# A fused attention, feed-forward, convolution and mixture-of-experts kernel: another order of ScalarE, TensorE and VectorE in the last two pairs of batches, and the last four experts' weights loaded one by one

## The reference, cut to what matters

```python
x = x + jnp.tanh(g_xattn[1]) * _L1_xattn_ref(ctx_2048, ctx_2048, _layernorm(x), L1_xattn_ssm_kernel, L1_xattn_D, 8)
x = x + jnp.tanh(g_ffn[1]) * _L1_ffn_ref(_layernorm(x), gate_w, w_gate_up, w_down, ws_gate_up, ws_down)
...
logits = jnp.einsum('th,eh->te', x, gate_w)          # 2048 rows, 64 experts
scores = jax.nn.softmax(logits, axis=-1)
topk_w, topk_ids = jax.lax.top_k(scores, 6)
topk_w = topk_w / (jnp.sum(topk_w, axis=-1, keepdims=True) + EPS)
...
routed = jnp.einsum('tef,ehf->th', jax.nn.silu(g) * u * comb[:, :, None], w_down)   # F = 176
shared = jnp.einsum('tf,hf->th', jax.nn.silu(sg) * su, ws_down)                     # 352
return routed + shared
```

## Time and profile before

| what | value |
|---|---|
| median of 3 runs | 728.07 us (726.86 to 729.16) |
| the profiled execution: its own time | 728.68 us |
| the profiled execution: span from first to last instruction | 726.9 us |
| mean granted clock of TensorE | 0.946 |
| TensorE busy (matmul) | 610.1 us, 84% |
| VectorE busy | 471.4 us, 65% |
| GpSimd busy | 450.9 us, 62% |
| ScalarE busy | 297.0 us, 41% |
| DMA moved | 163.69 MB, mean 225 GB/s |

### The profile page before, as it was taken

One profiled execution on the slowest core, in us unless ns is written; L12 is line 12 of the kernel. 1 busy time (PEld: TensorE's weight loads), 2 busy tenths in 40 slices (PEclk: granted clock), 3 DMA queues, 4 the chain that ended last, 5 costly groups with the idle time before them and its releaser, 6 DMA issues.

```text
span 726.9 us, 11813 instructions
## 1 busy us (share of the span) xinstructions
PE 610.1 (84%) x3072; PEld 470.3 (65%) x3072; DVE 471.4 (65%) x1596; ACT 297.0 (41%) x657; POOL 450.9 (62%) x512
## 2 busy tenths in 40 slices
PE   4698998769877989898747787999999999999930
PEld 3455554446666877787636566888888888887720
DVE  5898987998369898889764714245445545454425
ACT  3156777958233455455345121232322323233200
POOL 2697845782122478787766715477777777786560
PEclk9899999989999999999978989999999999999975
DMA  7578715869979843854223778899999999996868
GB/s 232 194 251 304 257 46 188 234 179 306 300 272 397 330 162 136 280 184 170 95 88 123 247 237 235 227 251 253 247 244 272 247 256 259 249 280 113 242 97 322
DMA packets 97822, 163.69 MB, mean 225 GB/s; under 512 B 10848, under 2 KB 65568, under 8 KB 96736
## 3 DMA queue, kind: packets, MB, share of 16 engines
q1 hardware_dynamic: 76864, 135.16, 56.6%
q0 software_dynamic: 20608, 27.82, 19.7%
q10 hardware_dynamic: 288, 0.01, 0.0%
HBM read 91.24 MB, written 71.71 MB: 224 GB/s over the span
## 4 chain that ended last, share of the span: by engine, by line
PE 56%; DVE 15%; issue 10%; DMA 7%; POOL 5%; ACT 3%; SPq 3%; DVEq 0%; POOLq 0%; ACTq 0%
PE psum L1159 11%; PE psum L1172 7%; PE psum L1163 5%; PE psum L899 5%; PE psum L1177 4%; PE psum L1043 4%; PE psum L1143 4%; PE psum L973 3%; POOL xs_rows L776 3%; PE psum L941 2%; PE psum L942 2%; PE psum L943 2%; PE psum L871 1%; DVE Z L1956 1%; DVE Z L1957 1%
## 5 line engine op out<-in xcount | busy, mean ns | idle before, releaser
L842 POOL DMA_INDIRECT acc<-hh,toki x128 | 188.0, 1469 | 87.4 <-DVE hh L2168 48.6
L2168 DVE TENSOR_SCALAR hh<-psum,wtok 96x256 f32<-96x256 f32 (+3 forms) x128 | 55.8, 477 | 131.9 <-issue 108.3
L776 POOL DMA_INDIRECT xs_rows<-Z,slot x96 | 100.9, 1051 | 38.8 <-issue 23.2
L1476 ACT ACTIVATE qT<-psum 128x384 f32<-128x384 f32 (+3 forms) x64 | 33.5, 524 | 98.0 <-PE psum L1143 97.1
L689 POOL TENSOR_TENSOR rstd<-mv,neghalf 128x1 f32<-128x1 f32 x48 | 32.5, 686 | 56.9 <-DVE mv L1915 38.2
L973 PE MATMUL psum<-wt,hh 128*128 128x256 f32 x256 | 59.2, 385 | 4.5 <-DVE mv L1915 3.4
L899 PE MATMUL psum<-wt,hTs 128*128 128x512 f32 x128 | 58.3, 597 | 0.6 <-ACT hTs L1255 0.6
L973 PEld LDWEIGHTS psum<-wt,hh 128*128 128x128 f32 x256 | 48.0, 193 | 11.3 <-ACT hh L1350 4.6
L1159 PE MATMUL psum<-qT,kve 128*128 128x192 f32 (+3 forms) x256 | 53.5, 353 | 0.0
L1482 ACT ACTIVATE H<-psum 128x192 f32<-128x192 f32 (+3 forms) x64 | 22.2, 348 | 66.1 <-PE psum L1159 65.4
L1043 PE MATMUL psum<-Z,wt 128*128 128x256 f32 (+1 forms) x192 | 48.2, 403 | 0.8 <-DVE H L2030 0.8
(11 more groups left out here) (368 smaller groups left out, 1428.9 us busy)
## 6 DMA issues: line engine op xcount, KB each, us to landing
xs_rows<-fill SPq DMA_DIRECT2D x64, 272.0 KB, 4.5
kve<-in_wexp SPq DMA_DIRECT2D x32, 496.0 KB, 4.2
Z<-in_wexp SPq DMA_DIRECT2D x30, 496.0 KB, 4.4
kve<-co_rows SPq DMA_DIRECT2D x8, 1376.0 KB, 7.1
kv_rows<-Z SPq DMA_DIRECT2D x8, 688.0 KB, 3.8
kve<-kv_rows SPq DMA_DIRECT2D x8, 688.0 KB, 7.8
Z<-xs_rows SPq DMA_DIRECT2D x24, 204.0 KB, 4.3
Z<-xs_rows SPq DMA_DIRECT2D x16, 272.0 KB, 3.8
```

Source lines behind the costliest of these rows:

```text
L776: pool.indirect_dma_start(out=xs_rows[:, :], out_offset=bass.IndirectOffsetOnAxis(ap=slot[:, t, k:k + 1], axis=0), in_=H[:, t, :], in_offs ...
L842: pool.indirect_dma_start(out=acc[a][:, :], out_offset=bass.IndirectOffsetOnAxis(ap=toki[0:p, g, j:j + 1], axis=0), in_=y_sb[0:p, s, j, :] ...
L2168: m = dve.tensor_scalar(y_sb[0:p, s, j, :], pY[par][0:p, j * D:(j + 1) * D], wtok[0:p, g, j:j + 1], None, ALU.mult)
```

## The change

It does three things.

1. On SyncE's queue, the loads of the last four experts' weights become a function `load_last(s)`, called after the first four of the six refill loops (after the experts' loops i = 0, 1, 2 and 3 to 4). The wait for all seeding is now at the head of the first of them. The wait `ov_ready` stays ahead of the first loop.
2. In the part written out for pairs 6 and 7, ScalarE makes the exponents of pair 5 before it copies the rows of pair 6, and normalises pair 6 before it makes the Silu of the shared expert's parts 0 and 1 of pair 5; the Silu of part 1 comes after the exponents of pair 6.
3. TensorE turns pair 6 and makes its logits after part 0 of the shared up-projection of pair 5, ahead of part 1. VectorE takes the second `times_q` of pair 7 before the shared expert's part 0, and part 1 after `place` of pair 6.

```diff
             for r in range(4, 6):
                 next_rows(r, r % 4, PARTS[0])
-            sp.wait_ge(seeded, 16 * (2 * NT + 3))
             sp.wait_ge(ov_ready, 2)
-            for s in range(4):
+
+            def load_last(s):
+                if s == 0:
+                    sp.wait_ge(seeded, 16 * (2 * NT + 3))
                 who = expert_at(E - 4 + s)
                 sp.dma_start(lastw[:, s, :], wexp[who]).then_inc(last_in, 16)
                 at = ODD * (s % 2)
                 sp.dma_start(lastd1[at:at + F1, s // 2, :], wd1[who]).then_inc(last_in, 16)
-            for lo_, hi_ in ((0, 1), (1, 2), (2, 3), (3, 5), (5, 6), (6, 7)):
+
+            for n_, (lo_, hi_) in enumerate(((0, 1), (1, 2), (2, 3), (3, 5), (5, 6), (6, 7))):
                 with sp.Fori(lo_, hi_) as i:
                     refill(i, PARTS[lo_], PARTS[lo_ + 1], WS if hi_ < E // WS - 1 else WS - 4)
+                if n_ < 4:
+                    load_last(n_)
...
             turn_q(2 * b + 1)
             shared_up(a - 1, 0)
+            r_turns(a)
+            logits(a)
             pe.wait_ge(qT_ready, NT)
             shared_up(a - 1, 1)
-            r_turns(a)
-            logits(a)
             shared_up(a - 1, 2)
...
             keep_logits(a - 1)
+            exponents(a - 1)
             keep_rows(a)
-            exponents(a - 1)
             query3(2 * b)
             evac_q(2 * b)
             query3(2 * b + 1)
             evac_q(2 * b + 1)
-            shared_silu(a - 1, 0)
-            shared_silu(a - 1, 1)
             normalise(a)
             evac_x(a)
+            shared_silu(a - 1, 0)
             keep_logits(a)
             exponents(a)
+            shared_silu(a - 1, 1)
             shared_silu(a - 1, 2)
...
             four(2 * b)
+            times_q(2 * b + 1)
             shared_hidden(a - 1, 0)
-            shared_hidden(a - 1, 1)
-            times_q(2 * b + 1)
             choose(a)
             four(2 * b + 1)
             weight_rows(a)
             place(a)
+            shared_hidden(a - 1, 1)
             shared_hidden(a - 1, 2)
```

## The result

| | before | after |
|---|---|---|
| median, us (6 runs each, same chip) | 727.82 (726.83 to 729.72) | 719.05 (713.72 to 722.97) |
| ratio, 95% interval | | 0.987 (0.982 to 0.991) |
| profiled execution, us | 728.68 | 720.17 |
| its span, us; mean granted clock | 726.9; 0.946 | 718.4; 0.944 |

The change is 1.3% faster, 8.8 us between the medians; 717.5 was forecast. Its lines stand five further down than before from TensorE's code on (L1159 is now L1164).

What follows compares the result with a forecast made beforehand. TensorE bounds the kernel from mid expert phase; before it, waits in GpSimd's scatters and SyncE's queue count. 5.9 us (loads) plus 4.7 (pairs) make 10.6, from 728.07 to 717.5 us; range 713.5 to 723.

Steps and rivals of the forecast that it cites:

- rivals in which one part pays nothing: Only the loads pay, 721.7 us, chance 0.12; or only the last pairs pay, 723.4 us, chance 0.08.
- the one in which nothing counts: Two late waits take the place of both removed ones: about 728 us, chance 0.03.
- lower end of the range, 713.5 us: Whole kernel: the time if TensorE's clock stays up through the pairs.
- Part 2: Last two pairs: moved exponents and pair 6's earlier order bring 4.7 us, bounds 2.5 and 5.4.
- step of the exponents: Pair 5: exponents ahead of keep_rows let GpSimd's first scatter go at 364.7 instead of 367.75, 3.1 us earlier.
- term for half clock at pair 6's turn and logits: Pair 6 on TensorE: turn and logits, if still at half clock, take an estimated 1.3 us more.
- bound of 5.4 us: GpSimd, pair 6: its own queue lets the first scatter come at most 5.4 us earlier.
- rule of the Trainium skill: ScalarE's moved Silu load: a 1.38 us drain besides the 1.28 us load would give 719 us; left out.
- Part 1: Expert phase: moving the last four experts' weight loads brings 5.9 us, bounds 3.2 and 6.4.
- 6.4 us for the stall and its clock: Expert 6 on TensorE: the 4.20 us stall goes, and 2.2 us of low clock after it.
- I take 0.5 us for both together: Starts after loops 2 and 3-4: waits of 0 to 1.6 us each for rows, bounds 0 and 3.2 together.
- rival "slower, DMA engines full": Expert phase: four loads cost 4.4 us each once rows behind them land after 6.0 us; 734.6 us, chance 0.04.

Runs made afterwards that it cites:

- all behind loop 0: The whole change, but all four loads of the last experts' weights stand behind the first refill loop: 727.49 us, ratio to before 0.999.
- no exponents: The whole change, but ScalarE's exponents of pair 5 stay behind the copy of pair 6's rows: 722.7 us, ratio 0.994; second run 724.38 us.
- numbers first: The whole change, with SyncE reading the first four experts' numbers ahead of its wait for the scatters: 716.2 us, ratio to before 0.979.
- second trace of before: The kernel before, profiled again with no edit: 724.47 us in its one run.
- pairs only: The kernel before with only the new orders of ScalarE, TensorE and VectorE in the last two pairs: 721.09 us, ratio 0.993.
- loads only: The kernel before with only the loads of the last four experts' weights moved: 723.29 us, ratio 0.994.
- loads and exponents: The whole change with TensorE's, ScalarE's and VectorE's new order of pair 6 undone: 719.81 us, ratio 0.987.

## Why the prediction was right, and where its sizes were off

**The sum.** Forecast 10.6 us, a ratio of 0.985. The three measurements of the change give 0.987, 0.989 and 0.986, 8 to 10 us. The stretches agree: P + E has a mean of 303.2 us in three traces of the change and 313.3 in two of before, 10.1 us less. The rivals in which one part pays nothing, and the one in which nothing counts, fall with the runs of each part alone. The total fits better than its parts, which is in part luck: by the means over all traces they are 4.9 and 4.4 us, 9.3 together. The lower end of the range, 713.5 us, follows from no sum of the prediction either: its upper bounds, 6.4 and 5.4 us, give 716.3.

**Part 2, 4.7 us forecast: 4.7 in the first two traces, 4.4 by means** (54.3 in three traces with the old order, 49.9 in eight with the new). The step of the exponents held to a tenth: table load ahead of the maxima, first scatter of pair 5 3.2 us sooner counted from the scatter before it, 3.1 forecast. The term for half clock at pair 6's turn and logits (1.3 us) wasn't paid in the trace of the change, 0.60 and 1.10 us. So the choice came 6.3 us sooner counted from pair 4's last scatter (382.00 - 363.05 before, 378.10 - 365.42 after), above the forecast 4.3 to 5.6. GpSimd's power of pair 7 came 4.8 us sooner by the same count (390.00 and 387.60), 4 to 5 forecast. What sets the end is then GpSimd's own queue, as the prediction's upper bound said. The bound of 5.4 us wasn't reached, since the queue itself got slower: from pair 5's first scatter to pair 6's it took 18.4 us, where the rows of before without their wait give 17.7, and three scatters in it took 1.05, 1.13 and 1.42 us, not 0.96. Why is open. In two traces with pair 6's new order the term was paid: P of 51.90 (all behind loop 0, clock 0.63 from 375 to 385 us) and 55.18 (no exponents, 0.50). The split, exponents 3.1 and pair 6 another 1.6, fits the runs with one move each: the order alone gave 1.7 us, and the exponents on top of it 3.0. The exponents alone gave 1.9, and the 1.2 us that TensorE's matmuls took longer in that trace account for the rest. What the prediction had too small is how far the clock moves this term: it allowed 1.3 us, and the two traces at half clock lost 2.6 us (55.18 - 52.63) and 2.3 us (51.90 less 49.58, the mean of the other seven with both moves).

ScalarE's moved table load for Silu took 1.28 us (376.05) and its Silu followed at 377.34 with no gap. The rule of the Trainium skill that was weighed there, in ScalarE: Activation LUTs (What ACT_TABLE_LOAD costs), would have put 1.4 us more before it; the trace has none, and leaving it out was right.

**Part 1, 5.9 us forecast: 4.9 by the means of E** (258.7 in three traces with the loads ahead of the loops, 253.8 in seven with one at each boundary, numbers first left out). Against before's first trace alone, on whose rows the forecast was made, it is 7.0 (260.5 - 253.5, the mean of the change's three). The term that was mis-sized is the 6.4 us for the stall and its clock, taken from one trace as if fixed. The stall was 4.20, 4.22 and 1.78 us, and from expert 6's to expert 8's transposes it took 11.23, 10.33 and 10.68 us where the change takes 9.0: the clock term is 2.2, 1.3 and 1.7. From the last scatter to expert 8's transposes, which holds both, the three traces took 46.7, 43.6 and 44.3 us and the seven a mean of 39.6, so the term is 5.3 us. The stall of 1.78 us in pairs only doesn't mean that the two parts overlap: expert 6's rows came as late as in the second trace of before, and TensorE, at its lower clock, came to them 2.7 us later.

**The waits at loop starts.** "I take 0.5 us for both together": from expert 8 to expert 63 the eight traces with one load at each boundary took 0.01, 0.41, 0.01, 1.37, 0.01, 0.51, 0.28 and 3.18 us more than before, a mean of 0.7. So the size was good, the bound (3.2) was reached, and one place was not: the prediction let only the boundaries behind loops 2 and 3-4 wait, and two of the waits came at expert 14, behind loop 0, where it had SyncE's delay swallowed by the wait for token numbers. The rival "slower, DMA engines full" had its mechanism right: where rows took 6.7 us and more to land behind a load (loads only), over its threshold of 6.0, TensorE waited. Its price of 4.4 us at each of four places was wrong: one load per boundary stays inside the room of the rows or just over it, two don't.

**The tail** took 48.8 us in the trace of before and 50.3, 49.4 and 49.7 in those of the change, its code untouched. Before's first trace has the shortest of all fourteen, which hides some 0.6 to 1.5 us of the gain in the comparison of the spans.

## What to carry to other kernels

When one engine's queue has two waits in a row, a move that feeds the second is worth only what the queue itself leaves: here pair 6's slots were early, and alone that gave 1.7 us, since GpSimd was still at pair 5's scatters. And read a term more than once before you trust its size: the same kernel gave 260.5 and 257.5 us for one stretch. Bulk loads that are moved off a dear place want to be spread, one at each place where the next transfer is issued with several microseconds of room; in this kernel one 0.54 MB load per boundary cost 0.7 us over all four boundaries, and four in one place cost 6 to 7.5 us, all that moving them had won. Before believing a difference of under 1%, cut the trace at events that both kernels share and compare the pieces, since the part that nobody touched moves too, here by 6.5 us ahead of the change's place and by 2 us behind it.

## What the runs showed of the hardware

- The same code up to the last pairs took 361.6 to 368.1 us. In the stretch of the last convolutions, 180 to 190 us, the granted clock was 1.00 in nine traces and 0.67 (after) to 0.91 in the other five. Single runs of one kernel spread likewise: loads and exponents ran in 713.5 to 723.7 us in ten runs, and of the runs of the kernel before beside numbers first the quickest had a span of 722.4 us at a mean clock of 0.947, the slowest 731.0 at 0.932. Why the clock falls in one run and not in another was not tried and stays open.
- A wait of TensorE costs more than its length if the clock falls with it, and that is not certain: 1.29 us before expert 30 in loads only cost 1.37 us, the 1.42 us before the same expert in numbers first cost 3.2 us, with a granted clock of 0.85 from 540 to 545 us and 0.81 in the five behind.
- A row load on SyncE whose expert number is read just before took about 1 us of the queue (4.05 us for four, 3.85 to 4.38 in the thirteen traces), and with the numbers in registers beforehand about half of it (1.90 us for four).
